# Cross-attention and quantised FFN: every context tile split, its remainders divided between GpSimd and VectorE

## The reference, cut to what matters

```python
q = (x @ Wq).reshape(b, n, 8, 64)
k = (context @ Wk).reshape(b, m, 8, 64)
v = (context @ Wv).reshape(b, m, 8, 64)
attn = softmax(einsum('bihd,bjhd->bhij', q, k) * SCALE)
x = x + einsum('bhij,bjhd->bihd', attn, v).reshape(b, n, 512) @ Wout + bout
# FFN: xq = fake_quant(layernorm(x)); h = fake_quant(silu(xq Wg) * (xq Wu)); x = x + h Wd
# fake_quant: one scale for the whole tensor, sigmoid(clip) * max|x| / 127; weights per row
```

## Time and profile before

| | us |
|---|---|
| median of 3 runs | 187.56 (186.99 to 190.17) |
| the profiled execution | 186.96 |
| its span, first to last instruction | 185.1 |
| TensorE busy | 179.0 (97%) |
| VectorE busy | 149.0 (80%) |
| GpSimd busy | 128.2 (69%) |
| ScalarE busy | 123.4 (67%) |

### The profile page before, as it was taken

One profiled execution on the slowest core, in us unless ns is written; L12 is line 12 of the kernel. 1 busy time (PEld: TensorE's weight loads), 2 busy tenths in 40 slices (PEclk: granted clock), 3 DMA queues, 4 the chain that ended last, 5 costly groups with the idle time before them and its releaser, 6 DMA issues.

```text
span 185.1 us, 2769 instructions
## 1 busy us (share of the span) xinstructions
PE 179.0 (97%) x883; PEld 141.1 (76%) x883; DVE 149.0 (80%) x319; ACT 123.4 (67%) x259; POOL 128.2 (69%) x112
## 2 busy tenths in 40 slices
PE   7999999999999999999999999999999999999983
PEld 3564687888888888788888988888889888876531
DVE  2896788899949974998999949989999419996784
ACT  3657978668866875778767747787667467753432
POOL 6398899799977775696866786968577877830110
PEclk9999999999999999999999999999999999999999
DMA  5746751233043101510341015200000000000001
GB/s 148 199 151 187 200 164 63 57 81 115 0 114 116 21 0 21 178 54 0 72 156 27 2 23 171 58 0 0 0 21 4 0 2 0 0 0 5 0 0 50
DMA packets 10262, 11.39 MB, mean 62 GB/s; under 512 B 6080, under 2 KB 8448, under 8 KB 10248
## 3 DMA queue, kind: packets, MB, share of 16 engines
q1 hardware_dynamic: 9816, 10.90, 20.6%
q10 hardware_dynamic: 432, 0.31, 0.5%
HBM read 10.97 MB, written 0.23 MB: 60 GB/s over the span
## 4 chain that ended last, share of the span: by engine, by line
PE 81%; DVE 12%; DMA 3%; issue 1%; SPq 0%; POOL 0%; ACT 0%; DVEq 0%; POOLq 0%; ACTq 0%
PE p_m L911 11%; PE p_sw L927 10%; PE p_sw L932 10%; PE p_sw L928 10%; PE p_n L957 8%; PE p_n L962 8%; PE p_n L959 8%; PE p_n L950 6%; PE p_n L968 3%; DVE w L722 3%; PE p_m L858 2%; DMA ctxT_in<-ctxT_d 2%; PE p_sw L1014 1%; DMA wqT<-wqT_d 1%; PE p_n L978 1%
## 5 line engine op out<-in xcount | busy, mean ns | idle before, releaser
L330 POOL TENSOR_TENSOR e_lo<-e_full,e_hi 125x448 fp32r<-125x448 f32 x80 | 105.8, 1333 | 31.2 <-ACT e_full L464 30.1
L609 DVE TENSOR_REDUCE chunk_max<-p_m 112x1 f32<-112x500 f32 x84 | 56.0, 672 | 16.7 <-PE p_m L911 16.0
L462 ACT ACTIVATE e_hi<-p_sw 125x448 fp32r<-125x448 f32 x80 | 43.5, 544 | 31.2 <-PE p_sw L932 30.8
L464 ACT ACTIVATE e_full<-p_sw 125x448 f32<-125x448 f32 x80 | 43.1, 539 | 0.0
L927 PE MATMUL p_sw<-q_hi,ctxT_lo 96*125 96x448 f32 x96 | 41.5, 432 | 0.0
L932 PE MATMUL p_sw<-q_hi,ctxT_hi 97*125 97x448 f32 x96 | 35.4, 369 | 0.0
L928 PE MATMUL p_sw<-q_lo,ctxT_hi 96*125 96x448 f32 x96 | 35.1, 365 | 0.0
L911 PE MATMUL p_m<-ctxT_hi,q_hi 96*112 96x500 f32 x84 | 32.4, 391 | 0.1
L957 PE MATMUL p_n<-e_hi,ctx_hi 125*128 125x448 f32 x80 | 29.5, 368 | 0.0
L962 PE MATMUL p_n<-e_lo,ctx_hi 125*128 125x448 f32 x80 | 29.2, 366 | 0.0
L959 PE MATMUL p_n<-e_hi,ctx_lo 125*96 125x448 f32 x80 | 29.1, 364 | 0.0
(11 more groups left out here) (227 smaller groups left out, 216.1 us busy)
## 6 DMA issues: line engine op xcount, KB each, us to landing
ctxT_in<-ctxT_d SPq DMA_DIRECT2D x7, 562.5 KB, 4.5
ctx_in<-ctx_d SPq DMA_DIRECT2D x8, 468.8 KB
ctx_nat<-ctx_d SPq DMA_DIRECT2D x8, 93.8 KB
ctxT_in<-ctxT_d SPq DMA_DIRECT2D x3, 187.5 KB, 3.3
q_hi<-maxima SPq DMA_DIRECT2D x28, 0.4 KB, 1.9
wqT<-wqT_d SPq DMA_DIRECT2D x2, 128.0 KB, 2.9
wout<-wout_d SPq DMA_DIRECT2D x1, 256.0 KB, 8.5
wkT<-wkT_d ACTq DMA_DIRECT2D x2, 96.0 KB, 2.3
```

What stands on the lines that cost most here:

```text
L330: pool.tensor_tensor(e_lo[:, k, :], e_full[:, k, :], e_hi[:, k, :], ALU.subtract)\
L462: act.activation(e_hi[:, k, :], p_s[n % 2][0:KT, 0:HQ], ACT.Exp, scale=SCALE)\
L464: act.activation(e_full[:, k, :], p_s[n % 2][0:KT, 0:HQ], ACT.Exp, scale=SCALE)\
L609: dve.reduce_max(chunk_max[:, c // NM, c % NM:c % NM + 1], p_mb[c % NM][0:GQ, 0:MC], AX.X)\
```

## The change

All 12 tiles are split now. `NATIVE`, `ctx_nat` and its loads are gone, `ctx_in`, `ctx_hi` and `ctx_lo` hold 12 tiles, and `weighted` does three passes for every tile. GpSimd subtracts `e_lo` for the six even tiles. For the six odd tiles ScalarE writes the full exponentials into the PSUM bank `p_x` and VectorE subtracts `e_hi` from it. There is one such bank, so ScalarE waits for VectorE's previous subtraction. GpSimd takes over from VectorE all `ctxT_lo` and `ctx_lo` splits, the latter in thirds.

The row of -1 is set by VectorE once and copied to the two other buffers by transfers. Three of batch 0's four rows of maxima go by transfers on SyncE's queue, each after a wait, ahead of `load_ctx(1)`. In the batch loop `load_ctx(b + 2)` comes ahead of `load_ctxT(b + 3)`; ScalarE takes the `ctxT_hi` splits one tile earlier. The weights are quantised in six steps between the tiles of the last batch. GpSimd does the Newton step of `layernorm2`. `project` uses `p_o[1]` instead of `p_x`. In the tail one spread of the maximum is left instead of two, and the last scaling of `attn` is in three pieces.

```diff
             load_ctxT(1)
             load_ctx(0)
-            load_nat(0)
+            sp.wait_ge(s.minus_made, 1)
+            for p in range(1, 3):
+                sp.dma_start(ctxT_hi[p][C:C + 1, :].bitcast(F32), ctxT_hi[0][C:C + 1, :].bitcast(F32)).then_inc(s.minus_copied, 16)
+            for g in range(G - 1):
+                sp.wait_ge(s.first_max_made, g + 1)
+                sp.dma_start(q_hi[C:C + 1, 0, g * GQ:(g + 1) * GQ].bitcast(F32), maxima[0][:, g:g + 1])\
+                    .then_inc(max_moved[0], 16)
             load_ctx(1)
-            load_nat(1)
...
             load_ctxT(2)
-            sp.wait_ge(s.ctx_lo_made, 2)
-            load_ctx(2)
             for b in range(B - 1):
-                move_max(b + 1, 0)
-                if b:
-                    sp.wait_ge(s.pv_done, T * b)
-                    load_nat(b + 1)
-                for g in range(1, G):
+                for g in range(G):
                     move_max(b + 1, g)
+                if b + 2 < B:
+                    sp.wait_ge(s.ctx_lo_made, 3 * (b + 1))
+                    load_ctx(b + 2)
                 if b + 3 < B:
                     wait_ctxT_lo(sp, b + 1)
                     load_ctxT(b + 3)
-                    sp.wait_ge(s.ctx_lo_made, 2 * (b + 2))
-                    load_ctx(b + 3)
...
+            for k in range(3):
+                split_ctx_lo(0, k)
             for n in range(T * B):
                 b, t = divmod(n, T)
-                if t in SPLIT:
+                if t in LO_POOL:
                     k = n % RING
                     pool.wait_ge(s.exp_made, 2 * n + 2)
                     pool.tensor_tensor(e_lo[:, k, :], e_full[:, k, :], e_hi[:, k, :], ALU.subtract)\
                         .then_inc(s.lo_made, 1)
+                if b == 0 and t in (0, 2, 4):
+                    split_q_lo(t // 2)
+                if b == 0 and t in (5, 7, 9):
+                    split_ctxT_lo(1, (t - 5) // 2)
...
+                if 0 < b < B - 1 and t in (1, 3, 5):
+                    split_ctxT_lo(b + 1, t // 2)
+                if 0 < b < B - 1 and t in (7, 9, 11):
+                    split_ctx_lo(b + 1, (t - 7) // 2)
...
+                act.activation(e_hi[:, k, :], p_s[n % 2][0:KT, 0:HQ], ACT.Exp, scale=SCALE)\
+                    .then_inc(s.exp_made, 1)
+                if t in LO_POOL:
                     act.activation(e_full[:, k, :], p_s[n % 2][0:KT, 0:HQ], ACT.Exp, scale=SCALE)\
                         .then_inc(s.exp_made, 1)
                 else:
-                    act.activation(e_full[:, k, :], p_s[n % 2][0:KT, 0:HQ], ACT.Exp, scale=SCALE)\
-                        .then_inc(s.exp_made, 2)
...
+                        act.wait_ge(s.lo_dve_made, lo_before(n, LO_DVE))
+                    act.activation(p_x[0:KT, 0:HQ], p_s[n % 2][0:KT, 0:HQ], ACT.Exp, scale=SCALE)\
+                        .then_inc(s.exp_made, 1)
...
-                if t in (5, 8, 11) and b + 2 < B:
+                if t in (4, 7, 10) and b + 2 < B:
                     split_ctxT_hi(b + 2, t // 3 - 1)
...
+            def e_lo_from_psum(n):
+                k = n % RING
+                dve.wait_ge(s.exp_made, 2 * n + 2)
+                dve.tensor_tensor(e_lo[:, k, :], p_x[0:KT, 0:HQ], e_hi[:, k, :], ALU.subtract).then_inc(s.lo_dve_made, 1)
...
+                    if n and (n - 1) % T in LO_DVE:
+                        e_lo_from_psum(n - 1)
...
-                if b == B - 1:
-                    quantise_weights()
+                    if b == B - 1 and t % 2:
+                        quantise_weights(t // 2)
+            e_lo_from_psum(T * B - 1)
             dve.reduce_max(xmax[:, 0:3], xh[:, 0:3, :], AX.X, apply_absolute_value=True).then_inc(s.xmax3_step, 1)
...
-                if t in NATIVE:
-                    j = NATIVE.index(t)
-                    if j == 0:
-                        pe.wait_ge(nat_loaded[b % 2], 16 * (b // 2 + 1))
-                    pe.wait_ge(s.exp_made, 2 * n + 2)
-                    pe.matmul(o[:, 0:HQ], ctx_nat[b % 2][:, j, :], e_full[:, k, :], start=(t == 0), stop=(t == T - 1),
-                              skip_group_check=True).then_inc(s.pv_done, 1)
-                    return
...
-            for g in range(G - 1):
-                if g == 0:
-                    pe.wait_ge(s.first_max_made, G - 1)
-                last = row(g)
-            last.then_inc(s.row_made, 1)
             query(4)
...
-            pe.wait_ge(s.xmax_step, 1)
             pe.wait_ge(s.sig_spread, 2)
-            pe.matmul(p_mb[0][:, 0:TOK], xmax[:, 2:3].to_broadcast([TOK, 128]), ident_sig[0][0:TOK, 0:TOK],
-                      start=True, stop=True)
+            busy(1, p_mb[1])
             busy(3, p_mb[1])
             project_last(PAIRS - 1)
```

More of the change, by code:

```diff
@@ L28 @@
 LAG = 3
[L29 to L32, removed]
+LO_POOL = tuple(range(0, T, 2))
+LO_DVE = tuple(range(1, T, 2))
+HALF_T = T // 2
+THIRD_T = T // 3
 FIRST_CHUNK_PLAN = (0, 1, 1, 1, 1, 1, 1, 2, 2, 2)
@@ L52, in chunks_at, with lo_before @@
     return [(b + 1, t + 2)]
-def splits_before(n):
-    return NS * (n // T) + sum(t < n % T for t in SPLIT)
+def lo_before(n, tiles):
+    return len(tiles) * (n // T) + sum(t < n % T for t in tiles)
 def program(nc, x_d, ctxT_d, ctx_d, wqT_d, wkT_d, wvT_d, wout_d, misc_d, wg_d, wu_d, wd_d, out_d):
@@ L102, in program @@
         ctxT_lo = [sb(f"ctxT_lo{p}", [C, M], F32R) for p in range(2)]
[L103 to L106, removed]
+        ctx_in = [sb(f"ctx_in{p}", [KT, T, C]) for p in range(2)]
+        ctx_hi = [sb(f"ctx_hi{p}", [KT, T, D], F32R) for p in range(2)]
+        ctx_lo = [sb(f"ctx_lo{p}", [KT, T, C], F32R) for p in range(2)]
         chunk_max = sb("chunk_max", [GQ, G, NM])
@@ L289, in _ @@
             pool.wait_ge(s.ident_made, 2)
-            pool.memset(ctxT_hi[0][C:C + 1, :].bitcast(F32), -1.0).then_inc(s.ones_made, 1)
-            pool.wait_ge(s.ones_made, 1)
+            for p in range(2):
+                pool.memset(ctx_hi[p][:, :, C:D].bitcast(F32), 1.0).then_inc(s.ones_made, 1)
+                pool.wait_ge(s.ones_made, p + 1)
             pool.wait_ge(s.ln0_step, 3)
@@ L318, in _, with split_q_lo @@
             pool.wait_ge(s.first_ctx_hi_made, 1)
-            for h in range(FULL_HEADS):
+            def split_q_lo(h):
                 pool.wait_ge(s.q_full_made, h + 1)
@@ L586, in split_q_lo @@
                                   q_hi[0:C, 1:B, heads_q], ALU.subtract).then_inc(s.last_q_lo_made, 1)
[L588 to L592, removed]
-                                  ctxT_hi[b % 3][0:C, key_piece(k)], ALU.subtract).then_inc(s.ctxT_lo_made, 1)
-            def split_ctx_lo(b, k):
-                if b == 0:
-                    dve.wait_ge(s.first_ctx_hi_made, 1)
-                else:
-                    dve.wait_ge(s.ctx_hi_made, 2 * (b - 1) + k + 1)
-                if k == 0 and b >= 2:
-                    dve.wait_ge(s.pv_done, T * (b - 1))
-                tiles = slice(k * HALF_S, (k + 1) * HALF_S)
-                dve.tensor_tensor(ctx_lo[b % 2][:, tiles, :], ctx_in[b % 2][:, tiles, :], ctx_hi[b % 2][:, tiles, 0:C],
-                                  ALU.subtract).then_inc(s.ctx_lo_made, 1)
             def chunk(b, c):
@@ L673, in normalise_last @@
                 invert()
-                for half in halves:
-                    rows(*half)
-                    scale(*half)
+                rows(*halves[0])
+                dve.wait_ge(step[0], 5)
+                scale(0, 2)
+                scale(2, 2)
+                rows(*halves[1])
+                dve.wait_ge(step[1], 2)
+                scale(4, 4)
             def residual(p, step):
@@ L967, in project @@
                 for h in range(H):
-                    last = pe.matmul(p_x[0:TOK, 0:D], attn[:, h, :, :].rearrange("c b i -> c (b i)"), wvo[:, h % 2, h // 2, :],
+                    last = pe.matmul(p_o[1][0:TOK, 0:D], attn[:, h, :, :].rearrange("c b i -> c (b i)"), wvo[:, h % 2, h // 2, :],
                                      start=(h == 0), stop=(h == H - 1))
@@ L1067, in _ @@
                     query(5 + t)
[L1068 removed]
+                if b == 1 and t == 9:
                     weights_vo()
```

248 lines of the change are left out of this document (130 added, 118 removed).

## The result

The changed kernel took 190.94 us, the median of 4 runs (189.56 to 191.04); the kernel before, run beside it, 187.28 (186.84 to 190.17, 4 runs). The ratio is 1.0185, 95% interval 1.0142 to 1.0229. I had forecast 185.9, range 183.2 to 188.6: wrong in sign and outside the range.

What follows compares the result with a forecast made beforehand. The prediction took TensorE to bound the kernel in the middle, other engines only at the ends. Terms -2.2 + 1.0 - 0.4 + 0.2 = -1.4 us gave 185.6 from the profiled 186.96; it put down 185.9, range 183.2 to 188.6.

Steps and rivals of the forecast that it cites:

- TensorE in the middle: Batch loop: 16 native tiles become split ones, each 0.14 us cheaper on TensorE, -2.2 us.
- four-pass sum: Native tiles on TensorE: four passes for true FP32 would save 0.20 us each, 3.3 us; not adopted.
- GpSimd, VectorE, ScalarE: Batch loop: their redistributed subtractions, splits and exponentials fit beside TensorE's work, 0 us.
- (C): Rival: GpSimd's or VectorE's order gets in the way in the middle; sum +0.2, 187.2 us; chance 0.12.
- The end: Tail: weights quantised between tiles let TensorE's first project matmul start sooner, -0.4 us (0 to -0.7).
- Quantising between the tiles: Last batch: quantising stands between VectorE's subtractions and may delay ScalarE and TensorE, +0.2 us (0 to 0.8).
- The startup: Startup: scores(0) 0.7 us earlier, but ctxT(2) lands at 26.9 to 27.0, delaying scores(7); net +1.0 us.
- (A): Rival: the startup does not lose, ctxT(2) lands by 25.3; sum -3.4, 183.5 us; chance 0.2.
- (B): Rival: ctxT(2) lands late, stopping ScalarE after exp(4); +2.1, 189.1 us at 30.5; chance 0.15.
- (D): Rival: native tiles were free, TensorE's path is not shortened; sum +0.8, 187.8 us; chance 0.03.

Runs made afterwards that it cites:

- experiment 8: Kernel before, each native tile's single float32 matmul replaced by three float32r passes on stand-in operands: 185.15, 185.42 us quick; 187.93, 188.47 slow.
- experiment 7: Changed kernel with ScalarE's ctxT_hi splits back at tiles 5, 8 and 11: ratio 1.0032; 187.51 and 187.62 us quick at full clock.
- experiment 12: Kernel before with SyncE waiting for the third first maximum ahead of load_ctx(1), run for its trace: 189.93 us, slow pace.
- experiment 4: Changed kernel with 12 filler matmuls on TensorE before scores(7): 187.71, 189.89, 190.61 and a disturbed 295.47 us.
- experiment 1: Changed kernel again, unchanged, ten executions: ratio 1.0049 to the kernel before; one untraced execution at clock 1.000 took 186.73 us.
- experiment 3: Changed kernel with load_ctxT(2) issued right behind load_ctx(1), ahead of the eight weight loads: 186.85 us median, ratio 0.9858.
- experiments 11: Kernel before with SyncE's wait for the third maximum ahead of load_ctx(1) and ctxT_hi split behind tiles 4, 7, 10: ratio 1.0114.
- 9: Changed kernel, all four maxima rows by TensorE and ScalarE, SyncE still waiting for the third maximum: 185.66 to 186.22 us quick, 188.48 to 188.95 slow.

## Why the prediction was wrong, by its steps

**TensorE in the middle**, -2.2: right. -2.0 between scores(12) and scores(95), in which 14 native tiles lie, is 0.14 each, and experiment 8 has it alone (-1.5 to -1.9; its scores groups 0.28 a batch). The trace decides against the four-pass sum of 0.20 a tile.

**GpSimd, VectorE, ScalarE**, 0: right. A pair of e_lo and ctxT_lo is 1.165 + 1.265 = 2.43 us, as the row of 1249 ns had it, and the subtraction out of PSUM took 614 ns for the 0.64 assumed:

```profile
L343 POOL TENSOR_TENSOR e_lo<-e_full,e_hi 125x448 fp32r<-125x448 f32 x48 | 55.9, 1165 | 32.7 <-ACT e_full L480 30.7
L634 DVE TENSOR_TENSOR e_lo<-p_n,e_hi 125x448 fp32r<-125x448 f32 x48 | 29.5, 614 | 4.6 <-ACT p_n L494 4.5
L321 POOL TENSOR_TENSOR ctxT_lo<-ctxT_in,ctxT_hi 96x500 fp32r<-96x500 f32 x21 | 26.6, 1265 | 1.6
```

Two means of the earlier trace rows were read as the work's own pace, and were not. GpSimd's e_lo has a mean of 1333 ns in before and 1165 here, for the same instruction, but a median of 1156 and 1154; the longest fell from 3.1 to 1.5 us. The long ones of before stand beside VectorE's splits (two in 4.25 us at 141.36, with L603 at 141.71 and 142.86), and those have moved. VectorE's 96x500 subtraction took 666 to 1509 ns, mean 955, so against the shortest of them GpSimd is 1.9 times slower, not 1.3. So the pairs of (C) had less to fear than their sum says.

**The end**, -0.4: right. From the last tile's end at 170.00 to the first projection matmul at 172.61 are 2.6 us, where the earlier trace rows give 3.0. TensorE is next late on the weight copies, 0.4, as foreseen:

```profile
171.51 1.04 PE L879 MATMUL p_m<-filler 128*128 128x512 bf16 x4 [0.43 <-ACT wdT L516]
```

**Quantising between the tiles**, +0.2: not seen. Batch 7's groups take 13.49 us for 13.79, less by its two native tiles.

**The startup**, +1.0: this is the step that failed; batch 1 started 3.6 us later than before. It had the right place and sign, and the wrong size in two parts.
First, the landing. I let `load_ctx(1)` go at 14.5 and its bytes start at 15.5; in experiment 7's trace, of the quick pace like the one I worked from, it went at 14.41. But I put ctxT(2) at 27.0, and it came at 28.11. I had taken the 12.0 us between two landings, ctx(0) at 14.85 and ctxT(2) at 26.89, as the time that the queue needs, and subtracted 0.7. The windows of the changed kernel show bytes for 12.25 us and a semaphore 0.5 after them. A landing is later than its last byte, so the 12.0 us began too late. The bytes show by how much. The loads of before up to and with ctx(0) are 2.32 MB, and the windows have moved that by 14.05 (165 GB/s); at 14.85 they have moved 2.39 MB, most of `load_nat(0)` too. (The same count comes out in experiment 12: the loads up to `load_nat(0)` are 2.42 MB, 161 GB/s for the 15 us by which the engines have run dry.) From 14.05 to the landing are 12.8 us, so 0.8 of the error is the start of the count. Most of the rest is the 0.7 taken off for fewer bytes: from the first bytes at 15.5 to the landing at 28.11 experiment 7's trace has 12.6 us, hardly less than before. The Trainium skill, DMA: Bandwidth & Descriptors (Anatomy of one DMA, SWDGE path), says of transfers issued from GpSimd that the semaphore waits until the last byte is confirmed in memory, and gives most of 2 us for it. These loads are issued by SyncE; they show the same order, with 0.5 to 0.8 us, and no run here shows what the gap consists of. At the slow pace scores(7) moved by 2.1 us, not 1.0.
Second, the clock. I priced the idle time and nothing behind it. After 2.7 us of idleness TensorE got 1.2 GHz from 34.2 to about 37.6, which is 1.5 us by experiment 4, and the odd execution of experiment 1 agrees. This term stood at nothing in the sum. It is most of what turned a gain into a loss: without it the measured sum is -0.4.

**The rivals.** (A) gave 183.5 if ctxT(2) is in time; experiment 3 makes it so, and takes 184.0 to 184.6. (B) has the right mechanism. I let its price grow with the landing alone, and so wanted a landing of 30.5 for +2.1; the changed kernel passed from gain to loss with much less, since the low clock came on top of the idle time. It deserved more than 0.15. (C) and (D) are excluded by the waits and by experiment 8. At the pace of the execution that I worked from, the changed kernel takes 188.2, 2.6 above the 185.6 of the sum: 1.1 by the landing and 1.5 by the clock. That is just inside the range, but on the wrong side of the kernel before. The rest of the distance to the first median of 190.94 is the startup's pace, for which the spread from 186.99 to 190.17 shown beforehand had been the sign.

## What to carry to other kernels

Here a wait put into a queue of loads was paid by the load at its far end. Find the first consumer of each load behind it, and move that load up, as here two lines did (experiment 3, 3.9 to 4.3 us). Before pricing a lateness, count how many tiles the bound engine is ahead, here 0.4 to 1.4 us for nothing; and where TensorE idles for some microseconds, look for a stretch at the lower clock behind it. Take the time that a queue needs from windows of bytes, not from the distance between two landings.

## What was not expected of the hardware

**Two paces of the startup.** TensorE's timeline of before, quick and then slow: the same three fillers take 0.83 and 1.50 us.

```profile
8.29 0.83 PE L858 MATMUL p_n<-filler 128*128 128x512 bf16 x3
```
```profile
10.17 1.50 PE L858 MATMUL p_n<-filler 128*128 128x512 bf16 x3
```

It is so for nearly all matmuls from 5.6 to 13 us, and scores(0) of before starts at 16.75 or 19.64. The granted clock stands at 1.00 in both, so the traces do not show whose doing it is. The Trainium skill, TensorE: Matmul & The Clock Gate (The HAM clock gate), says that how many of the first matmuls run at the low clock varies from run to run; that would fit, but no run here shows it.

**The lower clock comes late.** After the idle 2.74 us TensorE resumed at 32.54, and its granted clock fell only at about 34.2. In the second trace of the changed kernel the gap was 3.03 us, TensorE resumed at 32.99, and the clock fell at about 34.1. In the traces of experiments 11, 7 and 9, with gaps of 0.85, 1.1 and 1.5 us, the mean clock stayed at 0.998 to 1.000; the untraced executions of experiment 7 warn against taking that as a limit.
